# Roots spread over the partitions by single-pass products of a rounded high part and the rest

## The reference, cut to what matters

```
x = x + conv(groupnorm(x))                  # info and mask, outer product, 1x1 conv, relu
t = tokens(x)
t = t + attention(layernorm(t))             # linear attention: elu + 1, KV sums, then
        msg = layernorm(msg @ Wm, g1, b1)   #   (x - mu) * rsqrt(var + 1e-5) * g + b
        msg = layernorm(relu([x, msg] @ W1) @ W2, g2, b2)
t = t + experts(layernorm(t))               # top 2 of 8 experts by softmax, gelu, weighted sum
        top2_vals, top2_idx = top_k(softmax(logits), 2)
```

## Time and profile before

| | |
|---|---|
| time, median of 3 runs | 1175.86 us (1174.54 to 1176.95) |
| span of the profiled execution | 1171.7 us, 16823 instructions |
| the profiled execution's own time | not listed; only its span is |
| PE / PEld busy | 1058.5 us (90%) / 442.3 us (38%) |
| DVE busy | 740.2 us (63%) |
| ACT busy | 641.8 us (55%) |
| POOL busy | 361.7 us (31%) |
| mean granted TensorE clock | 0.985 of full speed |

### The profile page before, as it was taken

How to read it: one execution, slowest core, us unless ns; L and a number is a source line. 1 busy time by engine, 2 the same in 40 slices (tenths; PEclk the granted TensorE clock), 3 DMA queues, 4 the chain that set the end, 5 groups by cost and what they waited for, 6 DMA issues and landing times.

```text
span 1171.7 us, 16823 instructions
## 1 busy us (share of the span) xinstructions
PE 1058.5 (90%) x6646; PEld 442.3 (38%) x6646; DVE 740.2 (63%) x1529; ACT 641.8 (55%) x866; POOL 361.7 (31%) x280
## 2 busy tenths in 40 slices
PE   4798589979999899988999899998999989998898
PEld 1453244323533245332453235432453324532232
DVE  5744745686647875587664966468764886556344
ACT  3345355654566556664556546556556555665454
POOL 0000031333323333333232333133332342324465
PEclk9989889999999999999999999999999999999999
DMA  5000086007700284005810068000850039200760
GB/s 157 6 1 1 1 179 149 3 22 173 169 1 19 54 189 104 1 19 112 185 50 1 19 149 198 1 19 19 194 134 1 18 69 201 42 1 19 179 145 23
DMA packets 15597, 88.62 MB, mean 76 GB/s; under 512 B 3488, under 2 KB 6816, under 8 KB 11424
## 3 DMA queue, kind: packets, MB, share of 16 engines
q1 hardware_dynamic: 15520, 87.57, 32.3%
HBM read 78.12 MB, written 9.44 MB: 75 GB/s over the span
## 4 chain that ended last, share of the span: by engine, by line
PE 74%; DVE 12%; ACT 9%; issue 3%; DMA 1%; DVEq 0%; POOL 0%; POOLq 0%; SPq 0%
PE HP L847 15%; PE HP L861 14%; ACT H L992 5%; PE R L646 5%; PE R L621 4%; PE R L610 4%; PE R L699 3%; PE R L717 2%; PE R L708 2%; PE R L786 2%; PE R L795 2%; PE R L788 2%; PE R L861 2%; PE R L675 2%; DVE TM L1355 2%
## 5 line engine op out<-in xcount | busy, mean ns | idle before, releaser
L1044 POOL TENSOR_TENSOR XB<-TM,XB 128x512 f32<-128x512 f32 x254 | 323.0, 1286 | 658.5 <-DVE TM L1355 658.5
L992 ACT ACTIVATE H<-HP,W 128x1024 f32<-128x1024 f32 x224 | 243.0, 1116 | 205.7 <-PE HP L847 205.1
L1355 DVE SCALAR_TENSOR_TENSOR TM<-HP,B2S,CWB 128x512 f32<-128x512 f32 x224 | 163.2, 742 | 207.1 <-PE HP L861 196.3
L847 PE MATMUL HP<-XF,W1E 64*128 64x512 f32 x1024 | 269.9, 630 | 19.3 <-DVE TM L1355 18.5
L861 PE MATMUL HP<-H,W 128*64 128x512 f32 x896 | 233.1, 616 | 18.0 <-ACT H L992 18.0
L847 PEld LDWEIGHTS HP<-XF,W1E 64*128 64x128 f32 x1024 | 84.1, 187 | 143.9 <-DVE TM L1355 71.0
L861 PEld LDWEIGHTS HP<-H,W 128*64 128x64 f32 x896 | 48.5, 135 | 171.2 <-ACT H L992 116.3
L1156 DVE SCALAR_TENSOR_TENSOR BIG<-R,T 128x512 f32<-128x512 f32 x112 | 69.5, 681 | 20.9 <-PE R L610 20.8
L930 ACT ACTIVATE T<-R 128x512 f32<-128x512 f32 x96 | 57.4, 598 | 39.8 <-PE R L646 31.4
L958 ACT ACTIVATE T<-R,MINUS 128x512 f32<-128x512 f32 x64 | 41.4, 688 | 27.3 <-PE R L708 24.4
L1243 DVE SCALAR_TENSOR_TENSOR BIG<-T,R 128x512 f32<-128x512 f32 x64 | 41.8, 684 | 21.6 <-ACT T L958 21.6
(11 more groups left out here) (179 smaller groups left out, 1411.3 us busy)
## 6 DMA issues: line engine op xcount, KB each, us to landing
CWB<-gates_hbm SPq DMA_DIRECT2D x32, 1536.0 KB, 20.4
CWB<-gates_hbm SPq DMA_DIRECT2D x32, 512.0 KB, 6.6
out<-XB SPq DMA_DIRECT2D x15, 512.0 KB, 3.0
X<-x SPq DMA_DIRECT2D x14, 512.0 KB, 3.8
XF<-x SPq DMA_DIRECT2D x2, 512.0 KB, 6.1
gates_hbm<-RT SPq DMA_DIRECT2D x16, 64.0 KB, 1.6
W<-wpack SPq DMA_DIRECT2D x1, 968.0 KB, 4.9
W1E<-w1e SPq DMA_DIRECT2D x1, 512.0 KB, 7.4
```

The source lines that it names most:

```text
L847: last = mm(HP[u % BATCH][:, half(k)], W1E[img(k), e, :], XF[img(k), 1 - par, s, half(c)], start=True, stop=True)
L992: f(activated(b, u).rearrange("p k t -> p (k t)"), HP[u % BATCH][:, :], ACT.Gelu, bias=col(B1E + e))\
L1044: nc.gpsimd.tensor_tensor(acc, TM[:, u % BATCH, :], acc, ALU.add).then_inc(acc_done, 1)
L1355: v.scalar_tensor_tensor(out=TM[:, u % BATCH, :], in0=sums_of(b, u), scalar=B2S[:, e % 2, e // 2:e // 2 + 1], in1=CWB[:, s, e, half(c)], o ...
```

## The change

It does five things.

1. `root` waits for L1206 too, then copies the roots into the first half of a new tile `ROOT_HL` of type fp32r, waits, and subtracts that from the roots into the second half; this last operation raises `rs_done`.
2. `spread` makes 32 products for 16, in fp32r: those of the high part and of the rest add up in PSUM. `SPAN` becomes fp32r.
3. `SPAN` is loaded into the space of `RT` (`raw_span`) and rounded by one copy on ScalarE in the opening turn, after the copies of variance 2; the first spread waits for that.
4. `first_largest` works on one slot at a time (two operations of 128x128, the second not waiting for the first), with one table of 8 ranks read again and again; the table of 256 columns in `W` is cut to those 8.
5. The padded gate weights `GWZ` take the place of `wm_t`.

```diff
-NW_HELD = COLS["fold"][0]
+NW_HELD = COLS["rank"][0] + E
...
-        GWZ = sb("GWZ", [P, 3 * 2 * E])
...
-        SPAN = sb("SPAN", [P, NQ, P])
+        SPAN = sb("SPAN", [P, NQ, P], F32R)
...
+        ROOT_HL = sb("ROOT_HL", [P, 2, P], F32R)
...
+        raw_span = RT.rearrange("p g t -> p (g t)")[:, 0:NQ * P].rearrange("p (n c) -> p n c", c=P)
+        GWZ = w("wm_t")[:, 0:3 * 2 * E]
...
-                sp.dma_start(SPAN[32 * i:32 * i + 16, :, :], spans[0:16, :, :]).then_inc(span_in, 16)
-                sp.dma_start(SPAN[32 * i + 16:32 * i + 32, :, :], spans[32:48, :, :]).then_inc(span_in, 16)
+                sp.dma_start(raw_span[32 * i:32 * i + 16, :, :], spans[0:16, :, :]).then_inc(span_in, 16)
+                sp.dma_start(raw_span[32 * i + 16:32 * i + 32, :, :], spans[32:48, :, :]).then_inc(span_in, 16)
...
-                        pe.wait_ge(span_in, 16 * 2 * len(PIECES))
+                        pe.wait_ge(span_round, 1)
                     pe.wait_ge(rs_done, a * (LNS - 1) + k - 1)
                     pe.wait_ge(cp_done, copies(k) + len(PIECES))
                     for q in range(NQ):
-                        for i, (s, c) in enumerate(PIECES):
-                            rows = slice(32 * i, 32 * i + 32)
-                            last = mm(R[s][:, some_tokens(c, q)], SPAN[rows, q, :], ROOTS[rows, 3, :], start=True, stop=True)
-                            if q == NQ - 1:
-                                last.then_inc(ln_back[s], 1)
+                        for part in range(2):
+                            for i, (s, c) in enumerate(PIECES):
+                                rows = slice(32 * i, 32 * i + 32)
+                                last = mm(R[s][:, some_tokens(c, q)], SPAN[rows, q, :], ROOT_HL[rows, part, :],
+                                          start=(part == 0), stop=(part == 1))
+                                if q == NQ - 1 and part == 1:
+                                    last.then_inc(ln_back[s], 1)
...
                     for s, c in PIECES[:-1]:
                         kept(k, s, c)
+                    if starting(a) and k == 2:
+                        act.wait_ge(span_in, 16 * 2 * len(PIECES))
+                        f(SPAN[:, :, :], raw_span, ACT.Copy).then_inc(span_round, 1)
...
-                    v.scalar_tensor_tensor(out=y, in0=t, scalar=-2 / 3, in1=y, op0=ALU.add, op1=ALU.mult).then_inc(rs_done, 1)
+                    link(v.scalar_tensor_tensor(out=y, in0=t, scalar=-2 / 3, in1=y, op0=ALU.add, op1=ALU.mult))
+                    high = ROOT_HL[:, 0, :]
+                    link(v.tensor_copy(high, y))
+                    v.tensor_tensor(ROOT_HL[:, 1, :], y, high.bitcast(F32), ALU.subtract).then_inc(rs_done, 1)
...
-                    router_link(v.scalar_tensor_tensor(out=chosen, in0=values, scalar=0.0, op0=ALU.is_equal, op1=ALU.mult,
-                                                in1=w("rank").unsqueeze(1).broadcast_to([P, G, P])))
+                    ranks = W[:, COLS["rank"][0]:COLS["rank"][0] + E].unsqueeze(1).broadcast_to([P, 2 * TB, E])
+                    for s in range(G):
+                        count(v.scalar_tensor_tensor(out=rows(chosen)[:, s, :, :], in0=rows(values)[:, s, :, :], scalar=0.0,
+                                                     op0=ALU.is_equal, op1=ALU.mult, in1=ranks), router)
+                    dve.wait_ge(router, steps[router])
```

More of the change, by code:

```diff
@@ L299, in build @@
         span_in = sem("span_in")
+        span_round = sem("span_round")
         cp_done = sem("cp_done")
```

## The result

| | before | after |
|---|---|---|
| median of 4 runs, us | 1176.40 (1174.54 to 1177.51) | 1190.83 (1185.09 to 1193.07) |
| the profiled execution's own time, us | not listed | 1191.28 |
| span of it, us | 1171.7 | 1189.5 |
| mean granted TensorE clock | 0.985 | 0.975 |
| steady turn, us | 138.2 | 140.14 |

The ratio is 1.0113, 95% interval 1.0075 to 1.0152: the changed kernel is slower by 14.4 us between the medians, and by 17.8 between the spans. Forecast: 1191.0 (1184 to 1196).

A forecast was written before the change was run, and what follows sets the result against it. TensorE was taken to bound most stages, VectorE and ScalarE parts of the rest. Spreads 9.9 plus rank step 5.2 made 15.1 us on a span of 1171.7: 1186.8, plus 4.2 to the median: 1191.0 us, range 1184 to 1196.

The forecast's parts named there:

- The products: Spread on TensorE: 32 weight loads before and after, rounds stay at 111 ns, each spread 0.055 us shorter, not half.
- The sign: Spread rows on TensorE: the record was to be some 0.05 us shorter than 0.27, rounds still 0.11 us apart.
- The tail: Root's added copy and subtraction on VectorE, 0.59 us: costs 0.53, 0.59 and 0.14 at spreads 2, 3, 4.
- The split: Rank step L1291: waiting GpSimd sum goes before the second half; 0.64 in choose_1, 0.08 in choose_2, 5.2 us in all.
- rival 1: Split rank step: VectorE keeps its turn at the port, costing 1.3 us instead of 5.2; 1187.1 us; chance 0.32.
- The opening: Opening turn: first two spreads wait for the root, 0.53 us each; the third 0; split routing 0.16.
- The base: Whole run: the median's 4.2 us above the profiled span of 1171.7 was kept, taking 1186.8 to 1191.0.
- 2: Spreads: TensorE bounds, load rounds halve, each spread 0.50 us shorter with the root's tail covered; 1164 us; chance 0.04.
- 3: Spreads: narrow fp32r products stream twice as long, each spread 0.88 us longer; 1207.5 us; chance 0.07.
- 4: TensorE's idle time from 662 to 678 takes up the delays, nothing left of the turn's 2 us; 1176 us; chance 0.03.

The follow-up runs named there:

- products_only: Kernel after without the root's copy and subtraction and with the rank step whole, both parts reading one root tile: 1175.97 against 1173.99 us, turn 138.10.
- half_columns: Kernel after with 64 weight columns in place of 128 in the spread products: 1183.88 us, ratio 1.008, steady turn 139.90.
- tail_no_sums: Kernel before plus the root's copy and subtraction, without the two GpSimd sums beside spread 3: 1184.44 us, ratio 1.0064, turn 138.95.
- rank_split: Kernel before with only the rank step split into two operations: 1181.35 us, ratio 1.0053, steady turn 138.90.
- tiny_two_sources: Kernel before plus an 8-column VectorE operation with two SBUF sources behind each whole rank step: 1180.29 us, ratio 1.0049, turn 138.96.
- stacked: Kernel after with high part and rest in one tile's strips, 16 products a spread instead of 32: 1185.25 us, ratio 1.0089, turn 140.10.
- the one of 0.665: Trace of kernel before with the rank step split and one GpSimd sum beside choose_1 left out, TensorE clock 0.665 throughout: 1174.94 us, ratio 0.9997.

## Why the prediction was right, step by step

**The products** (0.055 us saved on a spread): right, 0.06. The mechanism, rounds paced by the load, is shown by products_only and half_columns. The sign by which I had meant to see it was wrong: the record's own duration didn't fall below 0.27 us (medians 0.268 to 0.271 in both); the 0.06 comes from the first round, where the second product of a strip started 0.16 us after the first and not 0.21. The Trainium skill, "TensorE: Matmul & The Clock Gate", LDWEIGHTS, lets the load go by its columns at 1.2 GHz, by estimate 107 ns for 128 and 53 for 64. The time between load rounds agrees for 128 (111) and comes out higher for 64 (61).

**The tail** (0.53, 0.59 and 0.14; 1.26 a turn): right, 0.53, 0.57 and 0.13. In spread 3 the price is not the tail's own length but GpSimd's two sums, as forecast; without them the turn falls by 0.55 (tail_no_sums).

**The split** (0.64 and 0.08): right, 0.64 and 0.08 in rank_split, and 0.69 together when taken out of after. The choice between 5.2 and 1.3 us was the prediction's open point, and rival 1 falls: the second operation, be it of 128 or of 8 columns, comes behind the waiting sum. The Trainium skill, "SBUF — State Buffer", Who interferes with whom, calls the ports that VectorE shares with GpSimd an exclusive lock and says that the order of issue decides who blocks. The traces of after, rank_split and tiny_two_sources agree (2.20, 2.20 and 1.23 us), also where nothing lies between the two VectorE operations.

**The opening and the turns up to 373 us**: too small. By 373 us of before's time my terms give 4.5 us (15.1 less five turns of 1.98 and the last routing's 0.72); measured were 7.5. The second trace of after has 5.7 us there, so 1.9 of the 3 us differ between two executions of one program. The stretch from 18 to 39 us is chance and cost 0.7 us. The rest is not all chance: up to the opening's third spread the forecast has 1.1 us (0.53 twice), and the two traces 3.1 and 4.8. There TensorE's idle time before the first two spreads grew as forecast, by 0.58 and 0.60 us (1.99 to 2.57, 0.52 to 1.12), but both traces ran at 1.2 GHz from about the first spread on, where before did not, and in the first the spread itself took 1.97 us instead of 1.17, at a granted clock of 0.50. The prediction put the clock at nothing. What lowers it there isn't shown, only that it came with the tail or the new products in nine traces of nine and without them in none of four. The whole span of the second trace grew by 15.9, against 15.1 forecast.

**The base** (4.2 us between span and median): mis-sized. After's own time lies 1.8 us above its span; with as much around before's, its profiled execution took about 1173.5, below all its listed runs. The median came out at 0.2 us from the forecast because 2.7 us too little in the span (1186.8 for 1189.5) and 2.9 too much around it (4.2 for 1.3) nearly cancel. What is confirmed to a few hundredths is the turn, 1.94 for 1.98, so 13.6 of the 14.4 us between the medians; the rest of the median's agreement is luck.

**Rivals.** 2 falls by products_only (turn 138.10, not shorter by the 1.5 us that halved rounds would give) and by stacked: even half the products gave 0.05 us. 3 falls by the spread of 1.11 us. 4 falls by every turn: nothing of the delays was taken up, five turns in a row grew by 1.93 to 1.95.

Left open: what lowers the clock at the first spread, and how far the time at half clock, 31 to 68 us among the traces (the one of 0.665 aside), explains that kernels with equal turns differ by some us in their medians.

## What to carry to other kernels

A cheaper kind of product saves next to nothing where small products are paced by their weight loads: compare the time between load rounds with the streaming first, and count as well whether the engine behind (here VectorE with two combines queued) would let the gain through. An operation split in two, or one more operation of two SBUF sources, opens a boundary at which a waiting GpSimd sum goes first, for its whole length, so on a chain between sums one long operation is better than two short ones. Measure such changes by the steady turn, which repeated to some 0.03 us here where the clock stayed full, while whole runs of one kernel spread over as much as 13.

## What the runs showed of the hardware that was not expected

- A VectorE operation of 8 columns with two SBUF sources took 1.23 us beside a standing sum and 0.15 elsewhere; a memset in its place took 0.07.
- Later turns ran in part at 1.2 GHz in most kernels' traces, in every second turn of rank_split and in single ones of eight others, before among them, and in none of after's two. A turn with 3.4 us of it was 0.9 to 1.1 us longer, one with 6.8 us 2.2 to 2.4.
- The same program had 58 us at 1.2 GHz in one execution and 45 in another, with a whole stretch of 21 us at the opening in the one and not in the other. That stretch, where TensorE idled by turns, cost 0.7 us; 3.4 us at 42 us cost 1.7.
- 31 runs of the kernel before beside the last experiments lie between 1169.62 and 1182.62 us, 1.1%: a difference like this case's 1.1% needs several runs of each, or the turn.
